# A three-stage tile pipeline made one step shallower, in a cross-attention, attention and expert kernel on one core

## What is computed

```python
def xattn(q, k, v, Wq, bq, Wk, bk, Wv, bv):
    qp = q @ Wq.T + bq                      # 256 x 128
    kp = k @ Wk.T + bk                      # 25088 x 128
    vp = v @ Wv.T + bv                      # 25088 x 512
    z = sigmoid(qp @ kp.T / sqrt(128))
    return z @ vp
x = x + xattn(layernorm(x), ctx, ctx, ...)
x = x + attn(layernorm(x), ...)             # 16 heads, causal, rotary part, 256 rows
x = x + ffn(layernorm(x), ...)              # 8 experts, the best one per row
```

## Time and profile before

| | us |
|---|---|
| median of 3 runs | 621.76 |
| their range | 620.83 to 621.79 |
| the profiled execution's own time | 620.86 |
| its span in the profile | 619.0 |
| PE busy in the span | 587.0 (95%) |
| DVE busy | 455.6 (74%) |
| ACT busy | 378.6 (61%) |
| stream of tiles, from the first score to the end of the last values | 23.3 to 497.7 |
| end of values(0) in the chain of waits | 40.97 |
| one tile in the middle: first keys matmul at 301.98, that of the next tile at 311.60 | 9.62 |

### The profile page before, as it was taken

How to read it: one execution, slowest core, us unless ns; L and a number is a source line. 1 busy time by engine, 2 the same in 40 slices (tenths; PEclk the granted TensorE clock), 3 DMA queues, 4 the chain that set the end, 5 groups by cost and what they waited for, 6 DMA issues and landing times.

```text
span 619.0 us, 7617 instructions
## 1 busy us (share of the span) xinstructions
PE 587.0 (95%) x3008; PEld 494.6 (80%) x3008; DVE 455.6 (74%) x460; ACT 378.6 (61%) x435; POOL 8.4 (1%) x9
## 2 busy tenths in 40 slices
PE   4499999999999999999999999999999979997797
PEld 3388888888888888888888888888888847784796
DVE  4588778777787777877878778787787758876544
ACT  3666767667677676676766767667676535564321
POOL 0000000000000000000000000000000040000000
PEclk9899999999999999999999999999999997999799
DMA  8366856877557466564564655646555310000000
GB/s 340 139 248 257 343 212 235 319 266 319 222 208 289 173 237 229 184 265 187 223 244 171 264 199 211 245 181 254 207 202 199 132 77 2 0 2 1 0 1 35
DMA packets 17971, 116.36 MB, mean 188 GB/s; under 512 B 2256, under 2 KB 2704, under 8 KB 4624
## 3 DMA queue, kind: packets, MB, share of 16 engines
q1 hardware_dynamic: 17360, 115.29, 49.2%
q10 hardware_dynamic: 576, 0.59, 0.3%
HBM read 115.35 MB, written 0.52 MB: 187 GB/s over the span
## 4 chain that ended last, share of the span: by engine, by line
PE 90%; DVE 5%; ACT 2%; issue 1%; DMA 1%; DVEq 0%
PE ps L367 43%; PE ps L325 22%; PE ps L342 12%; PE ps L650 4%; PE ps L675 2%; PE ps L602 2%; PE ps L553 1%; PE ps L466 1%; PE ps L483 1%; DMA x_s<-in_x 1%; PE ps L583 1%; PE ps L627 1%; ACT w L567 1%; DVE qa L511 0%; DVE qa L523 0%
## 5 line engine op out<-in xcount | busy, mean ns | idle before, releaser
L367 PE MATMUL ps<-nh,zh 128*128 128x512 f32 x392 | 152.7, 389 | 0.0
L367 PE MATMUL ps<-nh,zl 128*128 128x512 f32 x392 | 152.6, 389 | 0.0
L367 PE MATMUL ps<-nl,zh 128*128 128x512 f32 x392 | 152.6, 389 | 0.0
L311 DVE TENSOR_TENSOR nl<-rawn,nh 128x2048 fp32r<-128x2048 f32 x49 | 112.3, 2292 | 28.6 <-ACT nh L309 28.6
L352 ACT ACTIVATE zf<-ps 128x512 f32<-128x512 f32 x98 | 58.6, 598 | 100.9 <-PE ps L342 95.1
L357 DVE TENSOR_TENSOR zl<-zf,zh 128x1024 fp32r<-128x1024 f32 x49 | 60.1, 1226 | 78.1 <-ACT zh L356 78.1
L252 DVE TENSOR_TENSOR tl<-rawt,th 128x2048 fp32r<-128x2048 f32 x47 | 107.4, 2285 | 0.0
L309 ACT ACTIVATE nh<-rawn 128x2048 fp32r<-128x2048 f32 x49 | 93.6, 1910 | 0.0
L250 ACT ACTIVATE th<-rawt 128x2048 fp32r<-128x2048 f32 x47 | 89.7, 1908 | 0.0
L367 PEld LDWEIGHTS ps<-nh,zl 128*128 128x128 f32 x392 | 73.6, 188 | 15.4
L367 PEld LDWEIGHTS ps<-nl,zh 128*128 128x128 f32 x392 | 73.6, 188 | 15.2
(11 more groups left out here) (159 smaller groups left out, 663.8 us busy)
## 6 DMA issues: line engine op xcount, KB each, us to landing
rawn<-in_ctxn SPq DMA_DIRECT2D x49, 1024.0 KB, 4.8
rawt<-in_ctxt SPq DMA_DIRECT2D x48, 1024.0 KB, 5.7
wd_s<-in_wd SPq DMA_DIRECT2D x2, 1024.0 KB, 7.9
wu_s<-in_wu SPq DMA_DIRECT2D x1, 2048.0 KB, 8.2
wg_s<-in_wg SPq DMA_DIRECT2D x1, 2048.0 KB, 8.0
rawt<-in_ctxt SPq DMA_DIRECT2D x2, 512.0 KB, 6.3
wv_s<-in_wvt SPq DMA_DIRECT2D x1, 1024.0 KB, 8.0
wq_s<-in_wq SPq DMA_DIRECT2D x1, 1024.0 KB, 8.0
```

The costliest lines, as they stand in the source:

```text
L311: Nl[b] = put("vector", lambda e: e.tensor_tensor(nl[b % 2][:], rawn[b % 2][:], nh[b % 2][:], ALU.subtract), [n_ld[b], Nh[b]] + [AV[k] for ...
L367: AV[b] = put("tensor", lambda e, z=z, n=n, i=i, j=j, r=r: e.matmul(bank(4 + r), z[:, j * T + r * P:j * T + r * P + P], n[:, j * D:(j + 1) ...
```

## The change

Five things.

1. The loop over b emits for PE scores(b), keys(b+1), values(b): the values follow the weights of the same step. For ACT and DVE it emits weights(b), key_parts(b+1), split_n(b+1), split_t(b+2). keys(1) and split_n(0) move ahead of the loop. At the end, scores(48) and weights(48) go between the halves of values(47).
2. GpSimd clears a bfloat16 tile wz first of all, and PE does 14 matmuls of 512 columns with it (into a bank that isn't in use) ahead of the transposes.
3. The activation that makes ACT load the Sigmoid table is moved from behind the projection of the queries to ahead of it. The low half `half_l(1, 0)` goes ahead of key_parts(0) on DVE.
4. The sums of z's rows: one DVE reduction adds zacc's four blocks into zsum (128x256), two matmuls by ones take the place of eight, and they stand after three quarters of values(48) instead of ahead of it.
5. The split of wu is emitted ahead of values(48) and of the copy of zcol, right behind the reduction.

```diff
+        WZ = put("gpsimd", lambda e: e.memset(wz[:], 0.0), (), "wz")
+        for k in range(14):
+            put("tensor", lambda e: e.matmul(bank(7), wz[:, 0:P], wz[:], start=True, stop=True), [WZ])
...
+        put("scalar", lambda e: e.activation(sq[0:1, 6:7], sq[0:1, 0:1], ACT.Sigmoid), [SQ0], "sgw")
         half_l(0, 1, T0[1])
...
-        def values(b):
+        def values(b, js=range(4)):
...
         keys(0, (2,))
         half_h(1, 0, t_ld[1])
-        put("scalar", lambda e: e.activation(sq[0:1, 6:7], sq[0:1, 0:1], ACT.Sigmoid), [SQ0], "sgw")
+        half_l(1, 0, t_ld[1])
         key_parts(0)
         half_h(1, 1, t_ld[1])
-        half_l(1, 0, t_ld[1])
         half_l(1, 1, t_ld[1])
+        split_n(0)
...
-        for i in range(1, NB + 2):
...
-                scores(i - 1)
-                if i < NB:
-                    keys(i)
...
-            if i >= 2:
-                values(i - 2)
-            if i <= NB:
-                weights(i - 1)
-            if i < NB:
-                key_parts(i)
-            if i <= NB:
-                split_n(i - 1)
-            if i < NB - 1:
-                split_t(i + 1)
+        keys(1)
+        for b in range(NB):
...
+            if b < NB - 1:
+                scores(b)
+                weights(b)
+                if b:
+                    keys(b + 1)
+                key_parts(b + 1)
+                split_n(b + 1)
+                if b + 2 < NB:
+                    split_t(b + 2)
+            if b < NB - 2:
+                values(b)
+            if b == NB - 2:
+                values(b, (0, 1))
+                scores(b + 1)
+                weights(b + 1)
+                values(b, (2, 3))
+        ZS = put("vector", lambda e: e.tensor_reduce(zsum[:], zacc[:].rearrange("p (j n) -> p n j", j=4), AX_X, ALU.add),
+                 [ZA[NB - 1]], "zs")
+        for WUP in parts_of(wu_s, wuh, wul, [DWU, KP[NB - 1]], "wu"):
+            pass
+        values(NB - 1, (0, 1, 2))
+        for r in range(2):
+            m = put("tensor", lambda e, r=r: e.matmul(bank(0)[:, r:r + 1], zsum[:, r * P:r * P + P], one_s[:],
+                                                      start=True, stop=True), [ZS, ONE, KPL[NB - 1]], "zs1" if r else None)
+        values(NB - 1, (3,))
+        ZR = put("vector", lambda e: e.tensor_copy(zcol[:], bank(0)[:, 0:2]), [m], "zr")
```

More of the change, by code:

```diff
@@ L84, in program @@
         zcol = sb("zcol", [P, 2])
+        zsum = sb("zsum", [P, T])
+        wz = sb("wz", [P, 512], BF16)
         one_s = sb("one_s", [P, 1])
@@ L359, in weights @@
                         [ZF[b], Z0] + ([ZA[b - 1]] if b else []), "za")
-        def values(b):
+        def values(b, js=range(4)):
             n_h, n_l = nh[b % 2], nl[b % 2]
-            for j in range(4):
+            for j in js:
                 for r in range(2):
@@ L399, in parts_of @@
                           tag + "l")
-        for i in range(1, NB + 2):
-            if i == NB:
+        keys(1)
+        for b in range(NB):
+            if b == NB - 1:
                 DWU = dma("sync", wu_s[:], wu, "dwu", t_rd[NB - 1] + t_rd[NB - 2])
-            if i == NB + 1:
                 DWG = dma("sync", wg_s[:], wg, "dwg", n_rd[NB - 1] + n_rd[NB - 2])
[L406 to L409, removed]
+            if b >= 2 and late:
+                n = 1 if b < NB - 4 else len(late)
+                for dst, src in late[:n]:
@@ L427, in program @@
-            if i >= 2:
-                values(i - 2)
-            if i <= NB:
-                weights(i - 1)
-            if i < NB:
-                key_parts(i)
-            if i <= NB:
-                split_n(i - 1)
-            if i < NB - 1:
-                split_t(i + 1)
+                late = late[n:]
+            if b < NB - 1:
[7 more added lines that the diff above has]
+                    split_t(b + 2)
```

## The result

The changed kernel takes 624.4 us (median of 7 runs, 623.15 to 624.91) against 621.76 before (median of 7, 620.83 to 622.02): ratio 1.0043, interval 1.0031 to 1.0055. It is slower by 0.4%. The profiled execution took 623.9, its span is 622.0.

The account below looks back on a forecast made before the run. PE was taken to bound the kernel, with a new wait on zl. The terms -3.6 - 1.2 + 5.8 - 0.6 = +0.4 us, from the median, gave 622.2 us, range 618.2 to 626.0.

Parts of the forecast that it names:

- the slower rivals: Tiles: zl wait costs the whole load, 626.0 us, chance 0.20; start: half-clock stretch on first values, 624.2 us, chance 0.13.
- What bounds: Tile loop: PE's three blocks hold 77% of the chain of waits; the change makes PE wait for this tile's zl.
- Part 1, order: Start: earlier table load saves 1.4 us, shorter idle time behind scores(0) saves 2.2 us; 3.6 us together.
- Part 1, clock: Start: warm-up matmuls and shorter idle places give back 1.2 of at most 4.6 us lost at half clock.
- Part 2, the wait: Steady tiles: third values matmul waits for zl, 0.12 us per tile, 5.8 us over 48 tiles.
- The rival of the dear wait: Steady tiles: the wait on zl costs the whole weight load, 0.20 us a tile, 626.0 us; chance 0.20.
- The hidden wait: Steady tiles: third values matmul starts with its weight load, 0.02 us a tile, 617.4 us; chance 0.13.
- Part 3, the end: End of stream: row sums save 1.4 us, DVE's later copy of the second bank costs 0.8; 0.6 us saved.
- The warm-up at no cost: Start: clearing wz on idle POOL and 14 warm-up matmuls, done before 8.2 us, cost nothing.
- The clock stays up: Start: warm-up raises the clock and shorter idle places never let it fall, 3.4 us more saved, 618.8 us; chance 0.12.

Follow-up runs that it names:

- the one without the wait: Changed kernel with the two zl passes last in each first quarter of values, two matmuls later; 613.01 us with warm-up matmuls, 613.67 us without.
- both mendings: Changed kernel with zl passes two matmuls later and two of wu's four low parts made on DVE behind the transposed copy; 612.39 us.
- the tail edit alone: Changed kernel with only two of wu's four low parts moved on DVE to behind the transposed copy of the result; 620.81 us.

## Why the prediction was right or wrong, point by point

The forecast was no measurable change, 622.2 us; the measured 624.4 lies 2.2 above and is slower by 0.4%, inside the range but in the case of the slower rivals.

- **What bounds.** Right: PE bounds, and the new bound per tile is zl's end.
- **Part 1, order.** Right. 1.4 us for the table load: 2.2 in the run with it alone, 0.8 of it clock. The idle place behind scores(0): from 20.83 to 22.60 and then 0.5 us in front of the third matmul, about as worked out (1.9 and 0.8).
- **Part 1, clock.** Too low by 1.5 us. I took 1.2 of 4.6 us; the start won 6.3 where order alone gives 3.6, so the clock gave 2.7. Of the two half-clock stretches only the one behind scores(0) stayed; the idle places between the halves of th(1) no longer brought one, until the table load was put back.
- **Part 2, the wait.** The mechanism and the wait itself (0.12) were right, the term was mis-sized. I priced a late weight load at the delay of one matmul, and 0.18 a tile was measured: 0.12 of wait and 0.06 in the slower spacing of the ten matmuls behind. 46 tiles gave 8.1 us, where 0.12 gives 5.5. The row that I took the price from shows the matmul behind the wait, and I didn't look at the ones after it. These 2.6 us alone are more than the 2.2 by which the forecast missed. What kept the miss at 2.2 is luck: the start won 1.5 more than priced and made up for most of what the end lost.
- **The rival of the dear wait** named the right place and the right size (0.20 a tile) with the wrong reason: not the load's full record, which would have moved the third matmul by 0.20. The point from which it decides, 0.14 a tile, was passed. The load itself was late by that much (0.24), but its matmul didn't wait for it to end.
- **The hidden wait.** It fell. The Trainium skill, TensorE: Matmul & The Clock Gate, section "Architectural detail: the array is 16× 32×32, not 1× 128×128", states that a matmul can begin before its weight load completes; here the waiting matmul began 0.11 us after its load, which agrees with a start before the record's 0.19 are over, but not with a start at once.
- **Part 3, the end.** Wrong by 0.9 us up to the projection. The sum had -0.6 and, for the waits of the last two tiles, +0.24; +0.5 was measured. The row sums gave the 1.4 (1.68 us before, 0.34 now, in the chain). But the reduction took 2.04 us instead of 1.23, so DVE copied the second bank at 500.33, 1.85 us after the last values, instead of 1.5; and from there the copy and the four transposes took 1.7 us and not 1.3, at the half clock in part. Then a half-clock stretch fell on the projection, 1.1 us longer than before, that the prediction didn't price. It had said "What follows is as before".
- **The warm-up at no cost.** Its matmuls ended in time (before the transposes at 8.13, as said). But over the whole kernel it brought nothing that the medians show in the changed kernel, and some 0.7 us in the one without the wait.
- **The clock stays up** fell as a rival for this kernel: one stretch in the first 35 us, one at the projection. Its state at the start does occur: the profiled execution with both mendings had no half-clock stretch behind the transposes in the first 48 us.

In sum: start -6.3 (predicted -4.8), tiles +8.1 for 46 of the 48 (predicted 5.5 for as many), end with the other two +0.5 (predicted -0.4), and +0.7 behind it (predicted 0).

## What to carry to other kernels

When a pipeline is made shallower, compare the cover (PE's work between the last input and the first use) with the whole chain that makes the operand, to a tenth of a microsecond, in the steady step: what is gained is won once, and what is short is paid in every tile. If it is short by less than a matmul or two, don't go back to the deeper pipeline: inside the block, put the passes that don't need the late operand first. Here the passes with zl, moved two matmuls later, turned a loss of 0.4% into a gain of 1.3% (of which 0.2 points are a projection at full clock, for which one execution stands).

Count the lateness of the weight load too, and not only that of its matmul: with 0.24 us the load was twice as late here.

## What the runs showed of the hardware that was not expected

- After a wait of 0.12 us on a weight operand, the following ten or so matmuls of 512 columns stand about 0.232 us apart instead of 0.227 (485.94 to 488.03 for nine distances at the last full tile); the tile grew by 0.06 us over the wait. With a wait of 0.35 us it grew by some 0.03 over the wait. With the passes two matmuls later it is 0.227 from the first on.
- The slower spacing isn't bound to a wait. In the trace of the kernel before, values(48) follow the 16 instructions of the row sums; their matmuls wait for nothing and still stand 0.231 apart at first (492.25 to 494.79 for eleven distances), at a granted clock of 1.00, and the block takes 5.61 us instead of 5.44. What the cause is stays open.
- A DVE reduction of 128x1024 to 128x256 over a stride took 2.04 us, where a subtraction of two operands over as many columns takes 1.23.
- Half-clock stretches aren't where they were after edits far away: without the warm-up, or with zl earlier in its block, the projection some 490 us later took 6.88 us instead of 8.28. That the edits did it isn't shown: one kernel's own executions differ as well (619.15 to 623.71 us, granted clock 0.992 to 0.986, for the kernel with the tail edit alone). Times of single variants carry 1 to 3 us of this, so that differences under some 2 us between variants were told by the rows of the place that was edited.
